# Twenty-six groups of two across a pair, and the row maxima transposed by VectorE

## The reference

```python
q = (x @ Wq).reshape(B, Nq, h, dh)          # h = 16 heads of dh = 64
k = (context @ Wk).reshape(B, Nk, h, dh)
v = (context @ Wv).reshape(B, Nk, h, dh)
scores = einsum('bqhd,bkhd->bhqk', q, k) / sqrt(dh)
attn = softmax(scores, axis=-1)
out = einsum('bhqk,bkhd->bqhd', attn, v).reshape(B, Nq, h * dh)
return out @ Wo + bo
```

## Time and profile before

| | us |
|---|---|
| median of 3 runs | 1377.65 (1377.4 to 1378.37) |
| the profiled execution | 1379.35 |
| its span | 1377.5 |
| TensorE busy | 1299.5 (94%) |
| VectorE busy | 1025.2 (74%) |
| GpSimd busy | 893.9 (65%) |
| ScalarE busy | 806.6 (59%) |

### The profile page before, as it was taken

The page is one execution under the profiler, slowest core; times in us unless marked ns, Lnnn a source line. Parts: engine busy times, 40 slices in busy tenths (PEclk is TensorE's granted clock), DMA queues, the critical chain, the costliest instruction groups (busy, mean ns, idle before and its releaser), DMA issues. The chain is left out here.

```text
span 1377.5 us, 24906 instructions
## 1 busy us (share of the span) xinstructions
PE 1299.5 (94%) x8340; PEld 817.2 (59%) x8340; DVE 1025.2 (74%) x1676; ACT 806.6 (59%) x1093; POOL 893.9 (65%) x463
## 2 busy tenths in 40 slices
PE   7989999999999999999999999999999926999996
PEld 5655555555555555555455555555447915999996
DVE  5767878787887788788777877877977775666662
ACT  5456666666666666566566666666663213657753
POOL 3347876886787688779678877877687002445553
PEclk9999999999999999999999999999999956999998
DMA  9530010002001100200010010001313441545422
GB/s 258 200 128 10 25 42 31 17 18 63 17 24 31 45 17 17 60 21 17 26 57 17 16 57 24 17 17 63 127 53 116 162 155 58 142 133 128 105 37 28
DMA packets 75863, 88.83 MB, mean 64 GB/s; under 512 B 10555, under 2 KB 55644, under 8 KB 75740
## 3 DMA queue, kind: packets, MB, share of 16 engines
q1 hardware_dynamic: 68956, 78.32, 17.5%
q0 software_dynamic: 6784, 8.94, 4.0%
HBM read 58.98 MB, written 27.99 MB: 63 GB/s over the span
## 5 line engine op out<-in xcount | busy, mean ns | idle before, releaser
L919 POOL TENSOR_TENSOR acc_p<-acc_p,x_in 128x1024 f32<-128x1024 f32 x192 | 487.6, 2539 | 131.6 <-ACT x_in L1019 124.6
L100 DVE TENSOR_REDUCE mx_part<-ps_m 128x1 f32<-128x512 f32 x552 | 362.9, 685 | 178.5 <-PE ps_m L81 176.7
L1019 ACT ACTIVATE x_in<-ps_s 128x1024 f32<-128x1024 f32 x384 | 380.3, 1024 | 98.1 <-PE ps_s L835 71.3
L847 PE MATMUL ps_o<-x_in,v 128*64 128x512 f32 x1664 | 406.2, 606 | 0.3 <-DMA v<-v_scr 0.3
L824 PE MATMUL ps_s<-q,k 64*128 64x512 f32 x2496 | 386.4, 395 | 0.9 <-ACT x_in L1019 0.9
L824 PEld LDWEIGHTS ps_s<-q,k 64*128 64x128 f32 x2496 | 273.2, 185 | 41.7 <-ACT x_in L1019 6.6
L81 PE MATMUL ps_m<-k,q 64*128 64x512 f32 x736 | 211.6, 454 | 8.0 <-PEq L216 3.2
L847 PEld LDWEIGHTS ps_o<-x_in,v 128*64 128x64 f32 x1664 | 99.5, 136 | 180.9 <-issue 142.1
L81 PEld LDWEIGHTS ps_m<-k,q 64*128 64x128 f32 x736 | 99.5, 184 | 144.9 <-issue 100.8
L919 DVE TENSOR_TENSOR acc_d<-acc_d,x_in 128x1024 f32<-128x1024 f32 x96 | 174.8, 1821 | 5.8 <-ACT x_in L1019 5.5
L691 ACT ACTIVATE kept<-ps_m 128x512 f32<-128x512 f32 x184 | 109.6, 596 | 48.0 <-PE ps_m L81 45.3
(11 more groups left out here) (256 smaller groups left out, 1946.6 us busy)
## 6 DMA issues: line engine op xcount, KB each, us to landing
w_in<-in_w SPq DMA_DIRECT2D x16, 1024.0 KB, 5.1
v_st<-rec_scr SPq DMA_DIRECT2D x64, 128.0 KB, 2.9
o_scr<-v_st SPq DMA_DIRECT2D x32, 256.0 KB, 2.1
v<-v_scr SPq DMA_DIRECT2D x8, 832.0 KB, 5.3
v_scr<-c_in SPq DMA_DIRECT2D x10, 512.0 KB, 3.7
c<-o_scr SPq DMA_DIRECT2D x2, 1792.0 KB, 8.3
x_in<-in_x SPq DMA_DIRECT2D x4, 512.0 KB, 9.8
k<-o_scr SPq DMA_DIRECT2D x1, 2048.0 KB, 8.1
```

The costliest lines, as they stand in the source:

```text
L100: dve.tensor_reduce(part[:, j // S.MF, j % S.MF:j % S.MF + 1], bank[:, 0:S.MC], AX.X, ALU.max).then_inc(done or G.rough_used[hd], 1)
L847: last = pe.matmul(ps_o[hd * HP:hd * HP + DH, :], v[b][:, s, hd * DH:(hd + 1) * DH], probs[:, g % RING, hd * QC:(hd + 1) * QC], start=(s = ...
L919: eng.tensor_tensor(acc, other, probs[:, (u * KT + t) % RING, :], ALU.add).then_inc(done, 1)
L1019: act.activation(probs[:, g % RING, :], ps_s[:, g % 2, :], ACT.Exp, bias=G.pad_bias[:, 0:1] if s == KT - 1 else 0.0, scale=SCALE).then_inc ...
```

## The change

The 52 slots of a pair are walked through in 26 groups of two, without regard to units. So in units 0 and 2 (even) the groups are (0,1), (2,3) ... (10,11), then slot 12 together with slot 0 of the next unit, and in units 1 and 3 (1,2) ... (11,12). Where a group holds the last slot of a unit first, the values of that slot are computed in the group itself, and the next group computes one. The projection places in even units become slots 1 and 7 and the denominators' slot 3, so that they end a group. The copy of head 1's rough bank is made in the first slot of each group: 26 a pair, not 24. TensorE's transpose of the maxima and ScalarE's copy are gone: VectorE transposes them itself, in blocks of 32 x 32, behind its reduction (`turn_max`), four transfers place them in the row, and the row of ones holds -1 to turn the sign.

```diff
-KEPT = (0, 2, 5, 7, 9, 11)
...
+BLOCK, BLOCKS = 32, P // 32
 def place_mrow(sp, S, G, buf):
-    half = P // 2
-    for hd in range(2):
-        sp.dma_start(raw(G.m_rows[hd * half:hd * half + 1, buf, :]), raw(G.m_row[hd * S.QT:(hd + 1) * S.QT, :])).then_inc(G.mrow_placed, 16)
+    rows = raw(G.m_rows[0:P:P // 2, buf, :]).rearrange("o (t b r) -> o t b r", b=BLOCKS, r=BLOCK)
+    for i in range(BLOCKS):
+        sp.dma_start(rows[:, :, i, :], G.mx_t[i * BLOCK:i * BLOCK + 2 * S.QT, :]).then_inc(G.mrow_placed, 16)
+def turn_max(S, G, dve, unit):
+    dve.tensor_reduce(G.mx[:, 0:2 * S.QT], G.mx_part[:], AX.X, ALU.max).then_inc(G.max_ready, 1)
+    dve.wait_ge(G.max_ready, unit + 1)
+    if not (isinstance(unit, int) and unit == 0):
+        dve.wait_ge(G.mrow_placed, 16 * BLOCKS * unit)
+    dve.transpose(G.mx_t[:], raw(G.mx[:])).then_inc(G.mrow_ready, 1)
...
-                    pool.memset(raw(G.ones_row[hd * HP:hd * HP + 1, :]), 1.0).then_inc(s_ones, 1)
+                    pool.memset(raw(G.ones_row[hd * HP:hd * HP + 1, :]), -1.0).then_inc(s_ones, 1)
...
-GROUPS = ((0,), (1, 2), (3, 4), (5, 6), (7, 8), (9, 10), (11, 12))
-PROJ_PLACES = tuple((u, s) for u in range(UNITS) for s in (2, 8))
+PROJ_PLACES = tuple((u, s) for u in range(UNITS) for s in ((1, 7), (2, 8))[u % 2])
+DEN_PLACES = tuple((u, (3, 4)[u % 2]) for u in range(UNITS))
...
-DEN_SLOT, MROW_SLOT = 4, 10
 MAX_SLOT, REC_SLOT, NORM_ADD = 9, 7, 6
...
+        def jobs(p, g, head):
+            return MJOBS + MAHEAD + (p * SLOTS + g if head == 0 else p * GROUPS + g // 2)
+        def kept_jobs(p, g):
+            return p * GROUPS + (g + 1) // 2
...
             for hd in heads:
-                if hd and (j - 1) % MJOBS in KEPT:
-                    pe.wait_ge(kept_made, kept_count((j - 1) % MJOBS, unit if j else unit - 1) + 1)
+                if hd and g % 2:
+                    pe.wait_ge(kept_made, kept_jobs(p, g))
                 else:
-                    wait_for(pe, rough_used[hd], used_count(unit, j, hd))
+                    pe.wait_ge(rough_used[hd], jobs(p, g, hd))
...
-            dve.tensor_reduce(mx[:], G.mx_part[:], AX.X, ALU.max).then_inc(max_ready, 1)
-        def pe_maxt(pe, unit):
-            pe.wait_ge(max_ready, unit + 1)
-            pe.transpose(ps_x[0:NMU, 0:P], mx[:], G.ident[:]).then_inc(maxt_ready, 1)
-        def act_mrow(act, unit):
-            act.wait_ge(maxt_ready, unit + 1)
-            wait_for(act, mrow_placed, 32 * unit)
-            act.activation(m_row[:], ps_x[0:NMU, 0:P], ACT.Copy, scale=-1.0).then_inc(mrow_ready, 1)
+            turn_max(S, G, dve, unit)
...
-            for u in range(UNITS):
-                for n, group in enumerate(GROUPS):
-                    rough(u, group[0])
-                    for s in group:
-                        scores(u, s, then_rough=(s != group[0]))
-                    for s in GROUPS[n - 1]:
-                        values(u if n else u - 1, s)
-                    small(u, group[-1])
+            for g in range(0, SLOTS, 2):
+                rough(*divmod(g, KT))
+                for i in range(2):
+                    scores(*divmod(g + i, KT), then_rough=(i == 1))
+                joins_before, joins_here = (g - 2) % KT == KT - 1, g % KT == KT - 1
+                for n in range(g - 1 if joins_before else g - 2, g + 1 if joins_here else g):
+                    values(n)
+                for i in range(2):
+                    small(*divmod(g + i, KT))
```

More of the change, by code:

```diff
@@ L537, in _ @@
                 for n in range(13, len(vjobs)):
[L538 to L541, removed]
                     values(n)
@@ L664, in x_wait @@
[L664 to L674, removed]
+            users = [x for x in users if x[0] < (u, s)]
+            if not first:
+                users.append(((-1, 0), stage_lo, PROJ_JOBS * p - 1))
@@ L693, in dve_rough, with act_rough @@
-        def dve_rough(dve, j, unit, count):
+        def act_rough(act, j, p, g):
+            n = job_cols(j)
+            wait_for(act, kept_read, kept_jobs(p, g) - 1)
+            act.wait_ge(rough_ready[1], jobs(p, g, 0) + 1)
+            act.activation(kept[:, g // 2 % 2, 0:n], ps_m[:, 1, 0:n], ACT.Copy).then_inc(kept_made, 1)
+        def dve_rough(dve, j, unit, p, g):
             if j == 0:
@@ L831, in pe_minus_max @@
             if s == 0:
-                pe.wait_ge(mrow_placed, 32 * (unit + 1))
+                pe.wait_ge(mrow_placed, 16 * BLOCKS * (unit + 1))
             for hd in range(2):
@@ L935, in rough @@
                         pe.wait_ge(stage_lo, proj_count(made, PROJ_BLOCKS.index(("k", 3))) + 1)
-                    pe_rough(pe, 1 - b if other else b, (u + ahead) % UNITS, j, p * UNITS + u + ahead, heads)
+                    pe_rough(pe, 1 - b if other else b, (u + ahead) % UNITS, j, p, u * KT + s, heads)
             def scores(u, s, then_rough=False):
@@ L956, in scores, with values @@
                     pe_minus_max(pe, g, u, s, p * UNITS + u)
-            def values(u, s):
-                unit, g = p * UNITS + u, u * KT + s
+            def values(g):
+                u, s = divmod(g, KT)
+                unit = p * UNITS + u
                 if u >= 0:
@@ L966, in small @@
                 unit = p * UNITS + u
-                if s == DEN_SLOT and not (first and u == 0):
+                if (u, s) in DEN_PLACES and not (first and u == 0):
                     x_wait(pe, p, u, s, last)
@@ L1034, in copies @@
                     act_diff(act, DIFF_HI.index((u, s)), 1 - b, p)
-                if s == MROW_SLOT and not (last and u == UNITS - 1):
-                    act_mrow(act, unit + 1)
             def rough(u, s):
@@ L1041, in rough @@
                     j, ahead = job
-                    act_rough(act, j, p * UNITS + u + ahead, (p * UNITS + u + ahead) * MJOBS + j)
-            for u in range(UNITS):
-                for group in GROUPS:
-                    rough(u, group[0])
-                    for s in group:
-                        exponentials(u, s)
-                    copies(u, group[-1])
-                    if last and (u, group[-1]) in WO_HI:
-                        pairs = wo_pairs(WO_HI.index((u, group[-1])))
+                    act_rough(act, j, p, u * KT + s)
+            for g in range(0, SLOTS, 2):
+                rough(*divmod(g, KT))
+                for i in range(2):
+                    exponentials(*divmod(g + i, KT))
+                for u, s in (divmod(g, KT), divmod(g + 1, KT)):
+                    copies(u, s)
+                    if last and (u, s) in WO_HI:
+                        pairs = wo_pairs(WO_HI.index((u, s)))
                         act.wait_ge(wo_loaded, 16)
                         act.activation(G.wo_hi[:, pairs, :], wo_in[:, pairs, :], ACT.Copy).then_inc(wo_hi_done, 1)
-                    if last and (u, group[-1]) in AHEAD_HI:
-                        act_ahead(act, AHEAD_HI.index((u, group[-1])))
+                    if last and (u, s) in AHEAD_HI:
+                        act_ahead(act, AHEAD_HI.index((u, s)))
         def dve_pair(dve, p, b, first=False, last=False):
@@ L1062, in dve_pair @@
                 if s == MAX_SLOT and not (last and u == UNITS - 1):
-                    dve_max(dve, unit + 1)
+                    dve_max(dve, unit + 1, p, g)
                 if s == DVE_TILES[1] + 1:
@@ L1067, in dve_pair @@
                     j, ahead = job
-                    dve_rough(dve, j, unit + ahead, (unit + ahead) * MJOBS + j)
+                    dve_rough(dve, j, unit + ahead, p, g)
                 if s == REC_SLOT and not (first and u == 0):
```

60 lines of the change are left out of this document (25 added, 35 removed).

## The result

After the change the kernel takes **1390.06 us** (median of 6 runs, 1388.28 to 1392.48), the kernel before beside it 1377.87 (1377.2 to 1378.37): 1.0084 times as long, with an interval of 1.0074 to 1.0094. So it is slower by 12 us, 2 us under the 1392 of the prediction. The profiled execution took 1390.9 us, its span 1389.2.

What follows compares the result with a forecast made beforehand. TensorE's list of work was taken to bound the kernel, with VectorE having little room. Terms -6.2 - 3.2 + 1.0 + 15.3 + 5 + 3 = +14.9 us gave 1392 us as a median, range 1371 to 1410.

Steps and rivals of the forecast that it cites:

- start of the attention: Prologue: SyncE issues four placing transfers, not two, ahead of the last store of v, so the attention starts 1.0 us later.
- entering even units: Slot 0 gets partner slot 1, whose rough job waits on VectorE behind tile 11's sum: 5 us, bounds 0 and 20.
- entering odd units: Group (12,0): tile 11's sum stands between the reads of 12 and 0, late only if GpSimd holds it: 3 us.
- The walk through (8,9), unit 0: VectorE's operations inside (8,9), with block k0's projection, end at 5.4 us; TensorE wants the banks at 4.18, waits 1.3.
- The walk in unit 2: Same place with block k3's projection part (0.59 us): VectorE's readings end at 5.0 us, so TensorE waits 0.85.
- own sign of being wrong: Wrong if fronts after (8,9) come at 4.2 us, or if waits sit on the placed row or on ScalarE.
- Transposes: 31 transposes of row maxima leave TensorE's list at 0.20 us each, 6.2 us off; VectorE's transpose taken as 0.17 us.
- Groups: 28 groups a pair become 26, 16 fewer in 8 pairs, at 0.20 us each beyond their matmuls: 3.2 us off.
- The rival of sums locked out by waits: Waits push VectorE's sums onto GpSimd's, each costing 2 to 2.7 us, not 1.2: +51 us, to 1428; chance 0.06.
- All hidden: VectorE does its work under the values and only TensorE's list counts: -8.4 us, 1369 us; chance 0.17.
- Rows late: Four transfers of short rows land over 8 us after slot 9, so slot 0 waits: 1400 us; chance 0.05.
- Near balance: Low bounds hold, 9 us of waits at (8,9) and none at slot 0: +1 us, 1379; chance 0.12.

Runs made afterwards that it cites:

- The first experiment: The changed kernel with ScalarE's third copy of the tail of kw (third DIFF_KEEP entry) moved from slot 8 to slot 7 of unit 2; 1383.99 us, ratio 1.0034.

## Why the prediction came out right

| term | predicted, us | measured, us |
|---|---|---|
| TensorE's list: transposes and groups | -9.4 | about -15 (by difference) |
| start of the attention | +1.0 | -0.3 |
| (8,9) and behind it, even units | +15.3 | +22 |
| entering even units | +5 | +3 |
| entering odd units | +3 | 0 |
| sum | +14.9 | +9.7 (attention and its start: +10.0) |

The measured terms are worked out from differences of fronts. Free of waits, (8,9) takes 4.15, a plain group 3.92 and (0,1) of unit 2 5.52 (the lowest seen in the experiments). So unit 0 waits 0.61 + 0.58 and unit 2 1.29 + 0.59; seven pairs of 3.07 us, and 0.5 in the last one, make 22. Entering unit 2 is 0.45 seven times. With the waits taken off, units 0 and 1 would take 59.67 us for 60.56, and units 2 and 3 59.65 for 60.67: 1.91 us a pair, 15 for 31 units.

- **What bounds it, and where VectorE has no room: right.** The waits sit at the front of (10,11) in even units, on the readings of the rough banks, as said. The two kernels with added reductions show that place, not amount, decides. (The place that the prediction gave for how TensorE follows VectorE is no wait of its matmuls: the group before it lasted 4.78 us, like the others of its kind. A real one shows the same thing: head 0's reading of 592.66 ends at 593.34, and the weights follow at 593.40.)
- **The walk through (8,9), unit 0: right in kind and nearly in size.** 1.3 us predicted, 1.19 measured. It is split over two groups, because head 1's bank comes 0.6 us behind head 0's.
- **The walk in unit 2: wrong.** 0.85 predicted, 1.88 measured. The step "block k3 in u 2 (0.59), to 3.3" had no wait in it. I had moved the projection's place in my walk and not asked who else writes or reads its tile; `DIFF_KEEP` is in no line of the diff, and yet its slot fell behind the exponentials of the same group. The first experiment shows it. By its own sign of being wrong (waits on ScalarE) the prediction fails here in part: in unit 2 VectorE, and TensorE behind it, waited 1 us for ScalarE.
- **Transposes: right in size,** 0.21 us each in odd units. The Trainium skill's rule ("VectorE: DVE Perf Modes", Rules for kernel authors) is that VectorE is fastest for 32 x 32. The traces neither contradict it nor bear it out by much: VectorE's operation takes 0.21 us, TensorE's has a record of 0.27 but held the list for 0.20, and the shapes differ (128 x 32 and 128 x 8). It did not decide, since in even units VectorE's 0.2 us fell where nothing covered them. The pause ahead of it was 0.14 us (592.39 to 592.53), not 0.03.
- **Groups: mis-sized.** Two fewer a pair should have given 0.40 us. What is left of the 1.91, less four transposes (0.84), is 1.1. Between 0.2 and 0.3 of it is a wait that before had at (1,2) of unit 2, which lasts 4.65 or 4.72 us where a projection block 0.45 shorter than unit 0's should have made it 4.43. The weights of its second rough job wait there, in before:

```profile
628.39 0.18 PEld L81 LDWEIGHTS ps_m<-k,q 64*128 64x128 f32 x1 [0.43 <-DVE mx_part L100]
```

Another 0.2 is (4,5) being 0.1 shorter than (5,6), for which no row names a reason. The rest, 0.3 for each group against the 0.20 predicted, is not placed more closely, and no run changes the number of groups without moving VectorE's work, so its cause stays open.

- **Start of the attention: half the size, and hidden by chance.** SyncE's queue in the prologue of after, beside the earlier trace rows:

```profile
71.63 2.31 SPq L95 DMA_DIRECT2D m_rows<-mx_t  x4
73.98 0.40 SPq L267 DMA_DIRECT2D v_scr<-c_in  x1
77.18 1.60 SPq L810 DMA_DIRECT2D v<-v_scr  x2
```

The four transfers took 0.58 us each, not 0.70, and began 0.84 earlier, since the row comes without TensorE and ScalarE. From first transfer to store it went from 1.83 to 2.35 us, and from first transfer to first rough matmul from 5.02 to 5.58: 0.56 us for the predicted 1.0. That the attention nevertheless began 0.3 us earlier shows nothing: in four other kernels with this same prologue the first transfer came anywhere from 70.41 to 72.22, and the attention 5.6 us behind it.

- **Entering the units: too high.** Nothing waits at odd ones, nor at unit 0: tile 11's sum, which I took as held up there for 2.3 us, took 1.30 (568.11), for GpSimd's operation began behind it (568.29). At unit 2 the mechanism is there as predicted: tile 11's sum (628.96) takes 2.21 us beside a GpSimd operation of 2.35 from 627.74, and (0,1) waits 0.45. VectorE's sums over a stretch of the attention in after (minimum, median, maximum ns), beside the third line of the earlier trace rows:

```profile
L916 DVE TENSOR_TENSOR acc_d<-acc_d,x_in x24: 1207/1292/2225, 168.1 to 403.5; 128x1024 f32<-128x1024 f32 x24
```

Their median fell from 1960 to 1292 ns. The rival of sums locked out by waits went the other way, as its "against" said. That the kernel with its sums moved is slowed by 17.5 us shows how much hangs on the order in which the two engines happen to start.

- **The other rivals.** All hidden, 1369 us: refuted by the trace, though with k0 and k3 elsewhere 1374.80 is reached. Rows late: refuted by the doubled transfers. Near balance, 1379: refuted, and even without ScalarE's wait it is 1383.99.

That 1392 is within 2 us is in part luck, though the kind and the place of the main wait are right. The total is nearer than its terms were: the list became 5.6 us shorter than I had it and the entries and the start cost 6 us less, against waits that were 7 us longer, nearly all in unit 2 (1.03 more in each of seven); and the part behind the attention, which the change does not touch, ran 1.7 us longer in this profile. So two units in a row, for which 61.4 us was forecast, took 60.86 (0 and 1) and 61.98 (2 and 3).

## What to carry to other kernels

Fusing groups saves the busiest engine's changes of kind, but moves the work of the next engine against its deadlines: walk that engine's list between two deadlines at each new boundary, and beside it every tile that a moved operation writes, with whoever must read it first, even in lines that the diff leaves alone. An operation is free or paid in full by its place; the same 0.43 us cost nothing in odd units and 0.35 in each place in even ones. Before a VectorE operation with two SBUF inputs is moved, look at what GpSimd has in flight at the new place: the sum took 1.2 us where nothing was, and 2.8 to 3.0 where it was moved to.

## What the runs showed of the hardware

A wait of TensorE can be followed by a loss greater than its length. In the kernel with two more operations in even units, TensorE stood still 1.57 us ahead of a front of unit 2, and then the granted clock fell. Its windows (PE, PEld, DVE, ACT, POOL busy, granted clock, DMA share, GB/s):

```profile
284.20:286.70 2.50, 1.02 (x5) 0.65 (x7) 2.37 (x7) 0.00 (x0) 2.42 (x2) 1.00 0.01 1
286.70:289.20 2.50, 2.50 (x15) 1.49 (x13) 1.50 (x3) 1.93 (x3) 2.04 (x3) 0.58 0.01 1
289.20:291.60 2.40, 2.40 (x9) 0.64 (x8) 0.69 (x1) 0.71 (x1) 2.40 (x2) 0.73 0.00 0
291.60:294.00 2.40, 2.40 (x22) 1.65 (x20) 1.80 (x3) 1.66 (x2) 0.74 (x1) 1.00 0.26 100
```

For some 4 us the engine ran mostly at the lower of its two levels (0.58 and 0.73 in the mean), though it was busy throughout, and (10,11) took 6.08 us for 4.52. The wait was 1.56 to 1.64 us in all seven pairs with this place, and the clock fell in three of them (6.07 to 6.09 us), which cost 4.7 us; the attention's first group was 0.95 us shorter than in after, and together they make the 4 us that the readings did not explain. In after, where the wait is 1.23 us, (10,11) of unit 2 took 4.5 us in every pair. What tells the three places from the other four is not shown, and the length of the wait does not: it was 1.57 us in all three, and 1.56 to 1.64 in the four. In before TensorE stood still for 1.23 and 1.60 us at the start of two pairs (441.12 and 685.67), and the granted clock stayed at 1.00.
